# A two-layer block on one core: weight, fp8-slice loads and slice stores from ScalarE's queue, and the slot store ahead of the exponent load on SyncE

## What is computed

```python
x = x + attn(layernorm(x));  x = x + ffn(layernorm(x))
# attn: q, k (64 a head), v, g (128 a head), s = clip(x @ Ws, -32, 32)
z = cumlogsumexp(s);  g = exp(z_prev - z);  p = exp(s - z)
hk = hk * g_t + k_t p_t;  ok = q_t . hk;  pv = softmax(ok)
hv = hv * g_t + p_t v_t;  ov = pv_t . hv
o = rmsnorm(ov) * g_norm_weight * silu(x @ Wg);  out = o @ Wo
# ffn: y(x, w, scale) = (x @ fp8(w)) * scale
out = y(silu(y(x, gate_w)) * y(x, up_w), down_w)
```

## Time and profile before

| | us |
|---|---|
| median of three runs (lowest, highest) | 1346.76 (1345.14, 1353.50) |
| the profiled execution | 1354.85 |
| its span, from the first to the last instruction | 1353.1 |
| TensorE matmuls busy | 1333.3 (99%) |
| VectorE busy | 1050.0 (78%) |
| ScalarE busy | 428.9 (32%) |
| GpSimd busy | 136.8 (10%) |

### The profile page before, as it was taken

The page is one execution under the profiler, slowest core; times in us unless marked ns, Lnnn a source line. Parts: engine busy times, 40 slices in busy tenths (PEclk is TensorE's granted clock), DMA queues, the critical chain, the costliest instruction groups (busy, mean ns, idle before and its releaser), DMA issues.

```text
span 1353.1 us, 24406 instructions
## 1 busy us (share of the span) xinstructions
PE 1333.3 (99%) x9351; PEld 1107.6 (82%) x9351; DVE 1050.0 (78%) x1672; ACT 428.9 (32%) x1287; POOL 136.8 (10%) x106
## 2 busy tenths in 40 slices
PE   8999999999999999999999999999999999999998
PEld 7887888788878888888888888888888878888887
DVE  7887888788888888888888888888778875535354
ACT  4433323332333233223323332333333333222221
POOL 3001101110111011001200110011110010000000
PEclk9999999999999999999999999999999999999999
DMA  6157455655565556556555665566333430000000
GB/s 187 40 114 171 107 123 117 164 114 115 128 158 113 119 137 144 118 115 156 132 127 115 162 137 126 124 158 130 83 96 77 127 112 1 31 1 31 0 31 31
DMA packets 500559, 144.58 MB, mean 107 GB/s; under 512 B 359648, under 2 KB 491616, under 8 KB 500448
## 3 DMA queue, kind: packets, MB, share of 16 engines
q1 hardware_dynamic: 500448, 143.08, 45.4%
HBM read 85.80 MB, written 57.21 MB: 106 GB/s over the span
## 4 chain that ended last, share of the span: by engine, by line
PE 78%; DVE 8%; SPq 5%; DMA 5%; issue 2%; ACT 1%; DVEq 0%; ACTq 0%
PE bank L492 16%; PE bank L494 14%; PE bank L493 14%; PE bank L118 13%; PE bank L1752 6%; PE bank L734 3%; SPq L372 3%; PE bank L717 2%; PE bank L562 2%; PE bank L582 2%; SPq L336 1%; PE bank L722 1%; PE bank L653 1%; DMA fp_weights<-q 1%; DMA e_tokens<-k_tok_then_wT 1%
## 5 line engine op out<-in xcount | busy, mean ns | idle before, releaser
L492 PE MATMUL bank<-wvg_hi,xT_hi 128*128 128x512 f32 x512 | 207.7, 406 | 3.2 <-issue 2.5
L494 PE MATMUL bank<-wvg_hi,xT_lo 128*128 128x512 f32 x512 | 200.5, 392 | 0.0
L493 PE MATMUL bank<-wvg_lo,xT_hi 128*128 128x512 f32 x512 | 200.3, 391 | 0.0
L827 ACT ACTIVATE a_and_v<-bank 128x256 f32<-128x256 f32 x128 | 49.1, 384 | 334.2 <-PE bank L494 334.1
L492 PEld LDWEIGHTS bank<-wvg_hi,xT_hi 128*128 128x128 f32 x512 | 96.6, 189 | 28.0 <-issue 7.0
L494 PEld LDWEIGHTS bank<-wvg_hi,xT_lo 128*128 128x128 f32 x512 | 96.5, 188 | 20.7
L493 PEld LDWEIGHTS bank<-wvg_lo,xT_hi 128*128 128x128 f32 x512 | 96.9, 189 | 17.9
L1169 DVE RECIPROCAL cT<-cT 128x512 f32<-128x512 f32 x32 | 106.9, 3342 | 0.0
L1114 POOL TENSOR_TENSOR rstd<-ssq,neg_half 128x8 f32<-128x8 f32 x32 | 52.4, 1638 | 493.6 <-DVE ssq L1217 493.6
L492 PE MATMUL bank<-wo_hi,oT_hi 128*128 128x512 f32 x256 | 99.8, 390 | 0.0
L494 PE MATMUL bank<-wo_hi,oT_lo 128*128 128x512 f32 x256 | 99.6, 389 | 0.0
(11 more groups left out here) (181 smaller groups left out, 3056.7 us busy)
## 6 DMA issues: line engine op xcount, KB each, us to landing
o_transposed<-o SPq DMA_DIRECT2D x27, 512.0 KB, 3.4
oT_lo<-o_transposed SPq DMA_DIRECT2D x108, 128.0 KB, 3.0
fp_weights<-q SPq DMA_DIRECT2D x28, 318.0 KB, 3.1
e_tokens<-k_tok_then_wT SPq DMA_DIRECT2D x31, 256.0 KB, 2.3
e_tok<-e_tokens SPq DMA_DIRECT2D x124, 64.0 KB, 2.3
c_tokens<-cT SPq DMA_DIRECT2D x31, 256.0 KB, 2.4
cT<-c_tokens SPq DMA_DIRECT2D x124, 64.0 KB, 2.3
w_slots<-p SPq DMA_DIRECT2D x27, 256.0 KB, 2.4
```

What stands on the lines that cost most here:

```text
L492: pe.matmul(dst, w_hi, m_hi, start=(k == 0), stop=False)
L493: pe.matmul(dst, w_hi, m_lo, start=False, stop=False)
L494: last = pe.matmul(dst, w_lo, m_hi, start=False, stop=(k == n - 1))
L827: return act.activation(dst, src, ACT.Copy)
```

## The change

Five groups of moves go from SyncE's program to ScalarE's `unit`, as functions that take the issuing engine (`move_skq`, `move_vg`, `move_o`, `move_q8`, `move_q8_back`). Their waits go with them. Before the loop SyncE still issues them (the loads of pair 0, slice 0 in and out). In SyncE's loop w's load stands ahead of e's.

```diff
@@ SyncE's loop
         for u in range(1, UNITS - B + 1):
-            i, pair = (u - 1) % B + 1, (u + B - 1) // B
-            load_q8(u)
-            if i == 2:
-                load_skq(pair, 1)
             store_e(u + 1)
             if u in W_FAR:
                 store_w(u)
+                load_w(u)
             load_e(u + 1)
-            if u in W_FAR:
-                load_w(u)
             if u - 1 <= FAR:
                 store_o(u - 1)
             store_k(u + 1)
-            if i == 2:
-                load_skq(pair, 2)
-            if i == 3:
-                load_o(pair, 0)
-            if u == UNITS - B or (i == 1 and u > 1):
-                load_o(u // B, 1)
             if u - 1 <= FAR:
                 load_oT(u - 1)
             store_c(u + 1)
             load_k(u + 1)
             load_c(u + 1)
-            if i == 1:
-                load_skq(pair, 0)
-                load_vg(pair)
-            store_q8(u)
@@ ScalarE's unit
+            far = 1 <= u <= UNITS - B
+            pair = pair_of_next(u)
+            if 2 <= u <= UNITS - B + 1:
+                move_q8_back(act, u - 1)
...
             if u not in W_FAR and product_of(u) is not None and not last:
                 wT_evac(u)
+            if far:
+                move_q8(act, u)
+                if i == 2:
+                    move_skq(act, pair, 1)
             if projections:
                 split_next_w(1, nu, ni)
...
             if not last:
                 evac(VG0, nu, ni)
+            if far and i == 2:
+                move_skq(act, pair, 2)
+            if far and i == 3:
+                move_o(act, pair, 0)
+            if u == UNITS - B or (far and i == 1 and u > 1):
+                move_o(act, u // B, 1)
...
             if projections:
                 split_next_w(2, nu, ni)
+            if far and i == 1:
+                move_skq(act, pair, 0)
+                move_vg(act, pair)
             if not last:
                 evac(VG2, nu, ni)
```

More of the change, by code:

```diff
@@ L20 @@
 from contextlib import ExitStack
+from functools import partial
 import concourse.bass as bass
@@ L311, in out_bank, with move_skq, move_vg, move_o @@
         return (A[0], A[1], O[0], O[1])[c] if u == UNITS - 1 else (O[0], O[1], A[0], A[1])[c]
+    def move_skq(queue, pair, n):
+        if pair:
+            queue.wait_ge(s_wl, pair * 5 + n)
+        queue.dma_start(skq_stage(pair, n), (Ws, Wk, Wq)[n].rearrange("(k p) n -> p k n", p=P)[
+            :, :, bass.ds(pair * P, P)]).then_inc(s_stage if pair else s_stage0[n], 16)
+    def move_vg(queue, pair):
+        for k in range(KT):
+            if pair:
+                queue.wait_ge((s_vgl, s_vgl2)[k // 2], (pair - 1) * 2 + k % 2 + 1)
+            for n, w in enumerate((Wv, Wg)):
+                queue.dma_start(stage_vg[:, k, n * 2 * DV:(n + 1) * 2 * DV],
+                             w[P * k:P * (k + 1), bass.ds(pair * 2 * DV, 2 * DV)]
+                             ).then_inc(s_stage_vg[k], 16)
+    def move_o(queue, pair, a):
+        queue.wait_ge(s_wl, pair * 5 + 3 + a)
+        queue.dma_start(stage[:, :], Wo[bass.ds(pair * 2 * DV + a * DV, DV), :]).then_inc(s_stage, 16)
+    def slice_of(u):
+        return (0, QC0) if u == 0 else ((u - 1) * QC + QC0, QC)
+    def move_q8(queue, u):
+        if u == 0:
+            queue.wait_ge(s_xn, 3 * CH)
+            queue.wait_ge(s_xn2, CH)
+        else:
+            queue.wait_ge(s_fp8_out, 16 * u)
+        start, n = slice_of(u)
+        for m, w in enumerate(flat):
+            queue.dma_start(q8[:, m, 0:n], w[:, bass.ds(start, n)]).then_inc(s_q8in, 16)
+    def move_q8_back(queue, u):
+        queue.wait_ge(s_q8, Q8_STEPS * (u + 1))
+        start, n = slice_of(u)
+        queue.dma_start(fp8_scratch[:, :, bass.ds(start, n)].rearrange("n p c -> p n c"),
+                     q8[:, :, 0:n]).then_inc(s_fp8_out, 16)
     @block.sync
@@ L322, in load_x0 @@
                 sp.dma_start(y[:, c, :], x[0, P * c:P * (c + 1), :]).then_inc(s_x0[c], 16)
[L324 to L362, removed]
+        load_skq, load_vg, load_o, load_q8, store_q8 = (partial(f, sp) for f in (
+            move_skq, move_vg, move_o, move_q8, move_q8_back))
         def store_blocks(dram, tile, signal):
```

## The result

The changed kernel takes 1355.47 us in the median of 20 runs, the kernel before 1349.47 in 20 runs beside it: ratio 1.0042, 95% interval 1.0030 to 1.0053. That lies within the 1% named in the prediction, but on the slow side, above the predicted 1342 and above the range's upper end of 1353. One of the changed kernel's 20 runs lasted 4673.17 us and is left out of the ratio. The median before is now 2.7 us above the three-run median that the prediction started from, but that doesn't explain the miss: a gain of some 5 us was forecast, and a loss of 6 was measured. The profiled execution took 1358.87 us with a span of 1357.1, against 1354.85 and 1353.1 before.

The account below looks back on a forecast made before the run. SyncE's one order was taken to make w late and stall TensorE. Terms -13.6 + 1.0 + 3.9 = -8.7 us gave 1346.2 from the profiled run or 1338.1 from the median; the middle, 1342, was forecast, range 1333 to 1353.

Parts of the forecast that it names:

- What bounds the kernel: TensorE's stalls for w at L717 in i = 2 units, 8.8 us, plus half clock behind them, 4.8: 13.6 us removable.
- Loads and stores leave SyncE: In unit 6 SyncE waits for no weight or slice; Ws issued some 7 us earlier, VectorE's 3.09 us of idling go.
- w ahead of e: w's loads leave once its store has landed, freeing up to 2.35 us in unit 6; e's delay costs nothing.
- The stall that stays: Slice and Wk loads just before w's store leave 1.0 us of stall over all i = 2 units, bounds 0 and 8.8.
- Issues on ScalarE: At i = 1, nine issues behind Wo's split delay VG2's draining, `gate` and ST: 3.9 us in all, bounds 0 and 15.9.
- rival 3: Nine issues at i = 1 last 2 us longer through blocked issues, delaying VG2's draining and ST: 1355 us, chance 0.14.
- Slices later: Slice loads leave behind QT's copy; even if late, 2.7 us of cover before L734 needs VectorE's masks: cost 0.
- rival 4: Slices land 3.2 us later than put, beyond the cover, costing 0.5 us in 27 units: 1356 us, chance 0.04.
- Rival 1: Stalls go and issues on ScalarE cost nothing: 1333.2 us, or 1338 where a usual run loses less; chance 0.15.
- rival 2: Nothing moves: w is late through its transfers, not its place, so stalls stay in part: 1347 us, chance 0.17.
- the one I gave by the Trainium skill: All issuers end on the same 16 DMA engines, a second saves only issuing time: median would stay at 1346.8 us.

Follow-up runs that it names:

- the order alone: Kernel before the change with w's load moved ahead of e's and every DMA still on SyncE: 1340.17 us, ratio 0.9931; repeated 1340.81 us, 0.9931.
- run with an eighth of the bytes: Changed kernel with the loads of Wv and Wg of pairs 1 to 7 cut to an eighth of their columns, as many transfers: 1344.09 us, ratio 0.9955.
- the one with the loads spread: Changed kernel with Wv and Wg issued by ScalarE at the start of three units, two, two and four loads: 1347.37 us, ratio 0.9995.
- the queues alone: Changed kernel with e's load put back ahead of w's, all moves to ScalarE kept: 1353.44 us, ratio 1.0018 to the kernel before.
- the pair's loads alone: Kernel before with w's load ahead of e's, and only Ws, Wv and Wg moved to ScalarE: 1363.22 us, ratio 1.0102.
- the slices alone: Kernel before with w's load ahead of e's and only the slices' loads and stores on ScalarE, all weights on SyncE: 1343.12 us, ratio 0.9957.
- the pair's loads back on SyncE: Changed kernel with Ws, Wv and Wg again issued by SyncE behind the loads of k and c: 1347.41 us, ratio 0.9979.

## Why the prediction was wrong

**What bounds the kernel: half right.** The stalls for w in units with i = 2 and the half clock behind them were what was to be had: when they go, as in the order alone, the time falls by 0.69%, some 9 us. That answers what the prediction left open, how much of its 13.6 us a usual run loses: about 9. The cause was misplaced. I wrote that "SyncE's one order is what makes w late", with Ws, Wv, Wg, Wk and the slices in it. The runs show that e's loads ahead of w's suffice.

**Loads and stores leave SyncE: the step that failed.** The prediction has "Ws is issued some 7 us earlier" and counts only what that gives. It did give that, and more: Ws left 9.0 us earlier, counted from L717 and L706 (+3.97 us for +12.95). `oT_hi` came sooner, and VectorE's 3.09 us of idling fell to 0.99. But I never asked beside what those 1.25 MB would now pass. I weighed bytes only at w's store. The answer stood in SyncE's order: k's and c's transfers. The term is missing from the sum, that is, the sum has it at nothing: 12.2 us of waits at the key sums, some 11 of them by these bytes, and 2.6 us of half clock in the window behind the L706 of unit 13. The run with an eighth of the bytes takes it away (1.2 us left), and so does the one with the loads spread. In the profiled executions the shorter waits at L717, with their half clock, gave some 9 us, and this took some 15.

**w ahead of e: right, and worth more than I said.** I gave it up to 2.35 us of some 4 a unit and joined it to the queues; alone it brings all of the gain.

**The stall that stays: right in kind, too small.** I put 1.0 us; it was 2.7 us at L706, nearly all ahead of unit 2, with 1.6 us of half clock behind it. The slice's loads just ahead of w's store are part of it: moved earlier, w's store lands in 2.3 to 2.5 us in all units but one.

**Issues on ScalarE: right mechanism, wrong size here.** The sizes of its steps were right: nine issues took 4.34 us (226.37 to 230.71) for the 4.25 forecast. But I had the low part of Wo end at +5.5 us and Wo's load "0.3 us" later; issued by ScalarE ahead of L706, it landed sooner, and the low part ended at +3.9. `gate` ended at 231.93, 0.5 us before ST. So the term is 0 and not 3.9. It isn't a phantom: 2.9 us in the queues alone, 14 us in the pair's loads alone, which came close to the 15.9 of rival 3, though by a later low part of Wo and not by the blocked issues that rival 3 has.

**Slices later: nearly right.** VectorE waited for a slice in three or four units and not in most, so rival 4 fell. But the cost isn't 0: in unit 1 it is 1.1 to 1.3 us at the key sums. The 2.7 us of cover were read from the masks and L734. The work on c follows the slice's first step on VectorE too, and that path has hardly any cover: k's loads stand behind the store of c, and in unit 5 before, where they left at +8.50 us, the key sums already started 0.16 us late.

**The rivals.** Rival 1 fell with the new wait (its 4.6 us from 226.84 to 231.37 are 4.53), and so did rival 2 as worded, since the stalls did go. Rival 3 had the sign right and its mechanism wrong for this kernel; that its 1355 us are all but the measured 1355.47 is luck. The reading nearest to the result is the one I gave by the Trainium skill, DMA: Bandwidth & Descriptors, section Issuing engines are not separate DMA queues: whatever engine issues, the same 16 DMA engines carry it. I took it for "no gain"; with transfers that a product waits for on the same engines, it also means a loss. A DMA share of 1.04 to 1.24, k's issue of 3.03 us for 2.05, and 12.2 us of waits agree with it.

**What stays open.** The slices on ScalarE (+0.26% over the order alone) and Wk, Wq and Wo there (another 0.22%, between the slices alone and the pair's loads back on SyncE) are differences of runs whose intervals overlap or nearly touch. How the change would do with Ws alone on ScalarE wasn't tried, nor why units 0 to 2 and 13 suffer most, beyond the later leaving of k's loads in units 1 and 13.

## What to carry to other kernels

Reorder within the queue before moving anything to another one: here two lines gave 0.7%, and the new queue took all of it back. When a transfer starts earlier, look up what already passes in those microseconds and which product waits for it; its bytes are on the same DMA engines whoever issues them. An engine that works in order pays for each DMA that it issues or waits for with everything queued behind: price this from the time at which its last precondition is met, since 2.4 us there were the difference between nothing and 14 us.

## What the runs showed of the hardware that I had not expected

- An issue on ScalarE takes as long as one on SyncE: the nine of unit 5 took 0.39 to 0.52 us each and stood about 0.49 us apart (0.47 on SyncE). None of them blocked as the one of 2.42 us had the earlier trace rows.
- Large loads from a second queue stretch small ones of the first: the four loads of k in unit 5 (48 KB each) landed within 2.9 us before, within 5.5 in the changed kernel and within 5.8 with the pair's loads alone on ScalarE. Their issuing takes longer too, and so did one store of c, 2.10 us for 0.38.
- A stall of one length doesn't always cost the same: with the pair's loads alone on ScalarE, ST came 2.25 us late in units 17 and 21, and the granted clock fell and cost some 1.7 us more; in units 5 and 13 it came 2.20 and 2.26 us late, and the clock stayed at 1.00.
- Moving one load of 256 KB, Wk, some 7 us back cost about 14 us against the same kernel without the move, through an engine that is busy only a third of the time.
